# A sandwiched attention and feed-forward layer on eight cores: weight groups of 512 columns taken one at a time instead of in pairs, and the first LayerNorm in groups of three tiles

## The reference

```python
x = x + _layernorm(attn(_layernorm(x), qkv_w, proj_w, proj_b))
x = x + _layernorm(ffn(_layernorm(x), weight, gamma, beta, ln_weight, ln_bias))
# attn: 32 heads of 64, window of 8 tokens to each side with a distance mask,
#       softmax, times v, then out @ proj_w.T + proj_b
# ffn:  xn = layernorm(x) * ln_weight + ln_bias
#       out = xn @ sign(weight).T * max(abs(weight)) * gamma + beta
```

## Time and profile before

| | us |
|---|---|
| median of 3 runs | 1724.91 |
| lowest and highest | 1721.75, 1785.68 |
| the profiled execution | 1722.84 |
| its span, slowest core (core 4) | 1721.3 |
| spans of all cores | 1705.6 to 1721.3 |

### The profile page before, as it was taken

The page is one execution under the profiler, slowest core; times in us unless marked ns, Lnnn a source line. Parts: engine busy times, 40 slices in busy tenths (PEclk is TensorE's granted clock), DMA queues, the critical chain, the costliest instruction groups (busy, mean ns, idle before and its releaser), DMA issues. The chain is left out here.

```text
span 1721.3 us, 12664 instructions; the slowest of 8 cores (1705.6 to 1721.3 us)
## 1 busy us (share of the span) xinstructions
PE 932.3 (54%) x4372; PEld 436.7 (25%) x4432; DVE 570.5 (33%) x820; ACT 305.2 (18%) x438; POOL 306.9 (18%) x207
## 2 busy tenths in 40 slices
PE   1267777776395937766766761949100444249000
PEld 1123333333142413333333330424000222114000
DVE  3611111121202033333243222122527455640565
ACT  2400000000000013222232320000405221230121
POOL 0000000000000044654555540000000222200432
PEclk9998989999697965555555555979655666679555
DMA  3232322221802000000000008140586014040223
GB/s 101 98 123 101 117 100 98 98 98 57 285 1 98 1 28 1 0 1 0 1 0 1 1 0 258 60 147 1 169 290 248 6 43 147 1 146 1 98 97 146
DMA packets 37872, 140.57 MB, mean 82 GB/s; under 512 B 2082, under 2 KB 2082, under 8 KB 27170
## 3 DMA queue, kind: packets, MB, share of 16 engines
q1 hardware_dynamic: 34498, 117.61, 20.2%
q0 software_dynamic: 3312, 22.15, 3.2%
HBM read 122.98 MB, written 16.78 MB: 81 GB/s over the span
## 5 line engine op out<-in xcount | busy, mean ns | idle before, releaser
L379 PE MATMUL qk<-lnT,wbf 128*128 128x512 bf16 (+1 forms) x1254 | 254.5, 359 | 82.1 <-DVE wbf L40 80.2
L379 PEld LDWEIGHTS qk<-lnT,wbf 128*128 128x128 bf16 x1280 | 110.9, 101 | 225.7 <-issue 124.3
L446 PE MATMUL vp<-vwbf,lnT 128*128 128x512 bf16 x565 | 128.2, 388 | 57.1 <-DVE vwbf L40 56.5
L725 PE MATMUL dp<-pwbf,lnT 128*128 128x512 bf16 x501 | 113.9, 388 | 59.7 <-DVE pwbf L40 59.1
L969 PE MATMUL tpe<-identb,lnbf 128*128 128x128 bf16 x128 | 14.9, 308 | 225.0 <-DVE lnbf L955 221.3
L877 PE MATMUL ep<-fwbf,xnT 128*128 128x512 bf16 x500 | 117.5, 394 | 25.9 <-ACT fwbf L846 23.1
L486 POOL DMA_DIRECT2D maskm<-masks x1 | 0.7, 674 | 607.8 <-PE sp L510 607.8
L510 PE MATMUL sp<-KT,QT 64*128 64x144 bf16 x256 | 50.7, 274 | 107.2 <-DVE tstrip L525 101.1
L41 ACT COPY ptbuf<-tpc 128x512 bf16<-128x512 bf16 (+1 forms) x128 | 67.2, 577 | 180.9 <-PE tpc L603 180.9
L567 DVE TENSOR_REDUCE stats<-tstrip 128x16 f32<-128x2304 f32 x16 | 40.8, 2553 | 156.8 <-ACT tstrip L564 156.8
L535 POOL TENSOR_TENSOR tstrip<-tstrip,maskb 128x288 f32<-128x288 f32 x128 | 88.5, 727 | 6.6 <-DVE tstrip L525 6.6
(11 more groups left out here) (94 smaller groups left out, 1007.2 us busy)
## 6 DMA issues: line engine op xcount, KB each, us to landing
wstage<-qk_strips SPq DMA_DIRECT2D x32, 1024.0 KB, 5.9
vstage<-v_w SPq DMA_DIRECT2D x8, 2048.0 KB, 10.8
pwstage<-proj_wt SPq DMA_DIRECT2D x8, 2048.0 KB, 10.8
fwstage<-ffn_wt SPq DMA_DIRECT2D x8, 2048.0 KB, 13.4
ybuf<-y_scratch SPq DMA_DIRECT2D x16, 1024.0 KB, 7.7
xbuf<-x_shard SPq DMA_DIRECT2D x8, 1024.0 KB, 6.1
xre<-x_shard SPq DMA_DIRECT2D x8, 1024.0 KB, 10.6
y_scratch<-x POOLq DMA_DIRECT2D x8, 1024.0 KB, 9.2
```

Source lines behind the costliest of these rows:

```text
L379: return lambda e: e.matmul(banks[gi][:, 0:wd], wbf[:, par * D + kc * 128: par * D + (kc + 1) * 128], lnT[:, kc * TOK + c0: kc * TOK + c0 ...
L446: return lambda e: e.matmul(vbanks[bb][:], lnT[:, kc * TOK + 128 * vt: kc * TOK + 128 * vt + 128], vwbf[:, j * NGV + kc * 512: j * NGV + ( ...
L725: return lambda e: e.matmul(dbanks[bb][:], lnT[:, kc * TOK + 8 + 128 * t: kc * TOK + 8 + 128 * t + 128], pwbf[:, j * NGP + kc * 512: j * N ...
```

## The change

Stages 3, 5, 6 and 7 take one column group of 512 at a time. A pass over the token tiles now has 16 matmuls per tile, all into one bank, and there are two banks in place of four; the two halves of `vwbf`, `pwbf` and `fwbf` are used in turn, and each is released on its own. There are four passes where there were two. In stage 6 only group 0 is staged ahead and multiplied in the pair loop. Groups 1 and 2 follow behind the loop with a staging and a full pass each, then group 3's staging, the scale, and its pass in four pieces. Stage 1 has three buffers and takes the tiles in groups of three, three and two. The numbers of matmuls, weight loads, casts and DMAs stay as they were.

```diff
-            nc.sbuf_tensor("xbuf", [128, 2 * D], F32) as xbuf,
-            nc.sbuf_tensor("lnbf", [128, 2 * D], BF16) as lnbf,
-            nc.sbuf_tensor("sqdump", [128, 2 * D], F32) as sqdump,
+            nc.sbuf_tensor("xbuf", [128, 3 * D], F32) as xbuf,
+            nc.sbuf_tensor("lnbf", [128, 3 * D], BF16) as lnbf,
+            nc.sbuf_tensor("sqdump", [128, 3 * D], F32) as sqdump,
...
-            for bpair in range(0, NT, 2):
-                bs = [bpair, bpair + 1]
-                xas, lbs, cqs = [], [], []
-                for b in bs:
-                    par = b % 2
+            groups = [[0, 1, 2], [3, 4, 5], [6, 7]]
+            xbuf_rd_v = [xbuf_rd_v[0], 0, 0]
+            xbuf_rd_s = [xbuf_rd_s[0], 0, 0]
+            lnbf_rd_t = [lnbf_rd_t[0], 0, 0]
+            for bs in groups:
+                xas, lbs, cqs, pars = [], [], [], []
+                for idx, b in enumerate(bs):
+                    par = b % 3
...
-            nc.psum_tensor([128, 512], F32) as vp2,
-            nc.psum_tensor([128, 512], F32) as vp3,
         ):
-            vbanks = [vp0, vp1, vp2, vp3]
+            vbanks = [vp0, vp1]
...
-            for np_ in range(2):
+            for ng in range(4):
+                par = ng % 2
                 cast_last = 0
-                p.wait("v", "t", vwbf_rd_t)
-                for j in range(2):
-                    ng = np_ * 2 + j
-                    for hh in range(2):
+                p.wait("v", "t", vwbf_rd_t[par])
+                for hh in range(2):
...
                 p.wait("t", "v", cast_last)
...
-                    for kc in range(16):
-                        for j in range(2):
-                            def mk(vt=vt, kc=kc, j=j, bb=b0 + j):
-                                return lambda e: e.matmul(
-                                    vbanks[bb][:],
...
+                        def mk(vt=vt, kc=kc, par=par, bpar=bpar):
+                            return lambda e: e.matmul(
+                                vbanks[bpar][:],
+                                lnT[:, kc * TOK + 128 * vt: kc * TOK + 128 * vt + 128],
+                                vwbf[:, par * NGV + kc * 512: par * NGV + (kc + 1) * 512],
+                                start=(kc == 0), stop=(kc == 15))
+                        last_mm = p.emit("t", mk())
+                    eng = "v" if (vt % 2 == 0) else "s"
+                    p.wait(eng, "t", last_mm)
+                    if eng == "s":
+                        p.wait(eng, "g", c_zero)
+                    def mkevac(vt=vt, ng=ng, bpar=bpar):
+                        return lambda e: _copy(e, 
+                            VTOK[:, vt * D + ng * 512: vt * D + (ng + 1) * 512],
+                            vbanks[bpar][:])
+                    c = p.emit(eng, mkevac())
+                    bank_rd[bpar] = (eng, c)
+                vwbf_rd_t[par] = last_mm
```

The hunk for the output projection is the same edit with `dbanks`, `pwbf` and eight tiles. For the feed-forward stage:

```diff
-            ebanks = [ep0, ep1, ep2, ep3]
-            ebank_rd = [("v", 0)] * 4
+            ebanks = [ep0, ep1]
+            ebank_rd = [("v", 0), ("v", 0)]
...
-            def emit_ffn_mms(np_, tlist):
-                p.wait("t", "s", estate["sign_last"][2 * np_])
-                p.wait("t", "s", estate["sign_last"][2 * np_ + 1])
+            def emit_ffn_mms(ng, tlist):
+                par = ng % 2
+                p.wait("t", "s", estate["sign_last"][ng])
                 p.wait("t", "t", p.cnt["t"])
...
+                    eng = "v" if (t % 2 == 0) else "s"
+                    p.wait(eng, "t", mm_last)
+                    def mkev(t=t, ng=ng, bpar=bpar):
+                        return lambda e: _copy(e,
+                            ffnstage[:, t * D + ng * 512: t * D + (ng + 1) * 512],
+                            ebanks[bpar][:])
+                    c = p.emit(eng, mkev())
+                    ebank_rd[bpar] = (eng, c)
+                    ffn_rdy.setdefault(t, []).append((eng, c))
+                fwbf_rd_t[par] = max(fwbf_rd_t[par], mm_last)
 
             emit_ffn_stage(0)
-            emit_ffn_stage(1)
...
-            emit_ffn_stage(2)
+            for ng in range(1, 3):
+                emit_ffn_stage(ng)
+                emit_ffn_mms(ng, list(range(NT)))
             emit_ffn_stage(3)
...
             for tpair in range(0, NT, 2):
-                emit_ffn_mms(1, [tpair, tpair + 1])
+                emit_ffn_mms(3, [tpair, tpair + 1])
                 ffn_done_pair[tpair] = (p.cnt["v"], p.cnt["s"])
```

More of the change, by code:

```diff
@@ new lines, in build_program, with mkc @@
+                for hh in range(2):
+                    slot = (ng * 2 + hh) % 2
+                    p.wait("q", "v", stage_rd_v[slot])
+                    cq = p.dma("q", lambda e, ng=ng, slot=slot, hh=hh: e.dma_start(
+                        out=vstage[:, slot * NHV:(slot + 1) * NHV],
+                        in_=v_w.rearrange("(k pp) o -> pp k o", pp=128)[
+                            :, hh * 8:(hh + 1) * 8, ng * 512:(ng + 1) * 512]))
+                    p.wait("v", cq)
+                    def mkc(par=par, hh=hh, slot=slot):
+                        return lambda e: _copy(e,
+                            vwbf[:, par * NGV + hh * NHV: par * NGV + (hh + 1) * NHV],
+                            vstage[:, slot * NHV:(slot + 1) * NHV])
+                    cast_last = p.emit("v", mkc())
+                    stage_rd_v[slot] = cast_last
@@ L744, in build_program, with mk @@
-                pwbf_rd_t = mm_last
+                        def mk(t=t, kc=kc, par=par, bpar=bpar):
+                            return lambda e: e.matmul(
+                                dbanks[bpar][:],
+                                lnT[:, kc * TOK + 8 + 128 * t: kc * TOK + 8 + 128 * t + 128],
+                                pwbf[:, par * NGP + kc * 512: par * NGP + (kc + 1) * 512],
+                                start=(kc == 0), stop=(kc == 15))
+                        mm_last = p.emit("t", mk())
@@ new lines, in build_program @@
+                    p.wait("v", "t", mm_last)
+                    p.wait("v", projb_q)
+                    def mkev(t=t, ng=ng, bpar=bpar):
+                        return lambda e: e.scalar_tensor_tensor(
+                            x1[:, t * D + ng * 512: t * D + (ng + 1) * 512],
+                            dbanks[bpar][:], 1.0,
+                            projb[:, ng * 512:(ng + 1) * 512],
+                            ALU.mult, ALU.add,
+                            accum_out=accD[:, t * 4 + ng: t * 4 + ng + 1])
@@ L867, in emit_ffn_mms @@
                 for t in tlist:
[L868 to L871 removed]
+                    bpar = t % 2
+                    eng_r, cnt_r = ebank_rd[bpar]
+                    p.wait("t", eng_r, cnt_r)
                     for (eng_x, c_x) in xnT_rdy[t]:
@@ L874, in emit_ffn_mms @@
                     for kc in range(16):
-                        for j in range(2):
-                            def mk(t=t, kc=kc, j=j, bb=b0 + j):
-                                return lambda e: e.matmul(
-                                    ebanks[bb][:],
-                                    xnT[:, kc * 1024 + 128 * t: kc * 1024 + 128 * t + 128],
-                                    fwbf[:, j * NGF + kc * 512: j * NGF + (kc + 1) * 512],
-                                    start=(kc == 0), stop=(kc == 15))
-                            mm_last = p.emit("t", mk())
```

152 lines of the change are left out of this document (45 added, 107 removed).

## The result

| | before | changed |
|---|---|---|
| median, us | 1724.27 | 1681.52 |
| lowest and highest, us | 1721.75, 1785.68 | 1675.91, 1725.76 |
| runs | 10 | 10 |
| profiled execution, us | 1722.84 | 1678.68 |
| its span (slowest core), us | 1721.3 (core 4) | 1677.1 (core 7) |

The ratio is 0.9733, with a 95% interval of 0.9702 to 0.9763: the change is faster by 2.7%. The forecast was 1675 us, with a range of 1661 to 1692. In some executions the cores of one die show a lower granted clock (0.70 against 0.73 in the one of 1725.76 us) and take longer; medians count these, ratios and intervals leave them out.

The account below looks back on a forecast made before the run. No engine is full; a stage-to-stage chain with TensorE waits sets the end. Gains of 5.6 (first LayerNorm), 13.6 (V), 14.1 (output projection) and 14.6 (feed-forward) sum to 47.9 us: 1722.8 - 47.9 = 1675, range 1661 to 1692.

Parts of the forecast that it names:

- First LayerNorm: First LayerNorm: tiles in groups of 3, 3, 2 let the stage end 5.6 us earlier, bounds 0 to 8.
- V's start: V projection: the first pass needs two weight casts, not four, so it starts 12.5 us earlier.
- Pauses: Both projections: three pauses between passes, about 5.35 us each, replace one of 21.40 (V) or 21.93 (output projection).
- Restarts: Both projections: two extra restarts at the low clock behind pauses cost 2.1 us each, bounds 0 to 2.5.
- Output projection's start: Output projection: TensorE starts behind the second cast, at most at 1061.3 for 1073.96, a gain of 12.6 us.
- Feed-forward start (a): Feed-forward start: one weight group fetched ahead of the y tiles, not two; 12.4 us earlier, bounds 8 and 14.
- Front (b, c): Feed-forward front: (b) each of four pairs has 32 matmuls, not 64, gaining 27.6 us; (c) DVE's sums overlap TensorE, 3.6.
- Behind the front (d, e): After the front: (d) three stagings and passes cost 32.8 us; (e) the tail's first DVE product comes 3.8 earlier.
- 1: Rival: the clock outlasts pauses of 5 to 8 us, so six extra restarts cost nothing; 1662 us, chance 0.08.
- 2: Rival: loads bound the starts, so the first LayerNorm and the feed-forward start gain nothing; 1693 us, chance 0.12.
- 3: Rival: with two banks, late evictions pause TensorE and the clock drops within passes, costing 42 us; 1717 us, chance 0.06.
- 4: Rival: 16 matmuls in a row into one bank go at latency, 0.388 for 0.216 us; 1950 us, chance 0.04.

Follow-up runs that it names:

- filler: The changed kernel with 22 more matmuls, into an unread bank, behind each of the first three passes of both projections; median 1679.17 us, ratio 0.9681.
- four single-part kernels: Four kernels, each the kernel before with one part of the change (first LayerNorm, V projection, output projection, feed-forward); medians 1721.04, 1711.81, 1711.27, 1709.38 us.
- banks4: The changed kernel with four PSUM banks in turn again in V, output projection and feed-forward; median 1682.85 us, ratio 0.9715.
- combo: The changed kernel with projection casts inside the pass before, y tiles loaded first, and later feed-forward groups' signs and maxima moved earlier; median 1588.70 us, ratio 0.9216.
- only_vproj: The kernel before with only the V projection taking one column group at a time; median 1711.81 us, ratio 0.9875.

## Why the prediction was right, point by point

The forecast of 1675 against 1681.52 is off by 6.5 us; as gains, 47.9 was forecast and the medians differ by 42.8. The profiled executions differ by 44.2, the means of their eight spans by 47.1. Between the last two the gap is the choice of the slowest core: core 7, the slowest now, spanned 1721.2 before, and of its 44.1 us less its own tail took back 4.3 (126.1 to 130.4) where the others' moved by 0.2 on average. The mean of the eight cores itself was 1665.4 to 1671.4 in the executions of 1675.91 to 1684.34 us, so a gain read from one profile is good to a few us. The rows of the table sum to within about 1 us of their forecasts, and that is in part luck: single rows miss by up to 1.8 us, in both directions, and the misses nearly cancel. Step by step:

- **First LayerNorm, 5.6: too high by 1.7.** Most of this is the row I started from. The last pair began at 74.90 on core 4, but at 73.6 in the mean of eight cores. The changed kernel's groups began at 27.1, 50.2 and 69.7 in that mean where I had 26.9, 49.6 and 69.2, so the steps hold and the loads add half a us: 6.75 us passed from the first group's last apply to the second group's start, and I had let 5.8 pass. From core to core the stage gained 1.8 (core 3) to 7.0 us (core 4, the one I had read); a sum from one core's rows can miss by that much here.
- **V's start, 12.5: measured 12.6.** The first matmul stands 0.15 behind the second cast, as worked out.
- **Pauses, 5.35 each: exact but for one in V.** 5.35, 5.70 and 5.35 in V, 5.36 three times in the output projection. The weights were hidden, as the cast block at 477.14 shows.
- **Restarts, 2.1 each: right, and now known to be the clock.** The passes are 1.5 to 3.0 us above their pace, and `filler` takes 1.9 a pause back. Pauses and restarts together gave 0.0 in V for a forecast of 1.15, and 0.8 in the output projection for 1.5. The sentence "No pause of 5 us is in the trace" is true of the dense stages alone: in the attention of core 4, 15 pauses of 4.97 to 5.73 us stand ahead of matmuls of 64x144. These come four at a time, so the price of a restart of a long pass couldn't be read from them.
- **Output projection's start, 12.6: measured 13.3.**
- **Feed-forward start (a), 12.4: measured 13.5**, within its bounds.
- **Front (b, c), 31.2: measured 29.4.** (c) was exact: ACT's eviction started at 1312.27 and DVE's step at 1316.75, 4.48 behind (forecast 4.5). The three waits between pairs are 1.24 us shorter each, 3.7 together for 3.6. What was missed is in (b), "the cold part lies in the first 32, so it stays". In the mean of eight cores the four trains of 64 took 59.8 us, 4.5 above the pace of 55.3; the four of 32 take 34.2, 6.5 above 27.6. So 25.6 was gained and not 27.6. Windows of the first 32 matmuls of a pair (PE only, clock in the column behind the count), first of the kernel before, core 4, first and second pair:

```profile
1350.40:1359.60 9.20, 8.93 (x32) 0.77 0.00 0
1399.90:1408.30 8.40, 8.26 (x32) 0.85 0.00 0
```

  then of the changed kernel, the first pair on core 7 and on core 5:

```profile
1303.10:1312.20 9.10, 9.01 (x32) 0.78 0.00 0
1302.90:1310.60 7.70, 7.61 (x32) 0.92 0.00 0
```

  The same 32 matmuls take 7.6 to 9.1 us, as the granted clock has it. Before, core 4 got quicker from pair to pair (7.25 in the last, 14.16 - 6.91), while on cores 0 and 5 the last train of 64 was the longest, 16.1 behind 14.5. Now core 7 takes 9.01, 8.87, 8.79 and 8.76, and core 5 gets slower, from 7.65 to 8.58. So one core's rows don't give this term, and what sets the moment at which the clock rises in a train stays open.
- **Behind the front (d, e), -32.8 + 3.8 = -29.0: measured -27.5.** The pauses are 8.06 (forecast 8.1), each with a restart behind it, and the waits between pieces 0.26, not 0.37. The restart was less than I had it, 29.60 - 27.79 = 1.8 and 8.80 - 7.07 = 1.7 for 2.1. (e): the product stands 2.75 ahead of the last matmul's end (1549.42), forecast 2.7. The scale hid behind the fourth pass.
- **What doesn't change:** Q/K 0.3, attention 0.1, the LayerNorm behind the output projection 1.2, which no part explains: the four single-part kernels have 63.2 to 64.5 there.

The rivals: **1** (the clock outlasts the pauses, 1662) is refuted; a restart follows every pause of 5.35 and 8.06, and `filler` shows its price. **2** (starts bound by loads, 1693) is refuted for both starts: 13.5 us came where 12.4 was forecast, and 3.9 where 5.6 was; of the missing 1.7 the loads account for 0.5. **3** (two banks let the clock drop inside a pass, 1717) is refuted by `banks4`, and by the clock of 1.00 throughout a pass of `filler`. **4** (one bank's accumulation in a row runs at latency, 1950) is refuted: 144 matmuls, 16 in a row to a bank, took 31.24 us in `filler` and 128 took 27.79 in `combo`, 0.217 each.

## What to carry to other kernels

Halving the unit of work that must be staged took 12.6 to 13.5 us off each of three waits of 33 to 43, and that was 39 of the 47 us; the gain from more, shorter passes in the middle was nearly nothing, since each shorter pause was followed by a restart at the lower clock that cost about 2 us. The larger prize was in the order of one engine's list: the same casts placed between the evictions of the pass before, and not behind its last, took pauses and restarts away together, 41.6 us. Look which loads stand ahead of the first one needed, and cut the trace at the same marks on all cores where a few us matter: the slowest core's time moved by 8 us from run to run in the changed kernel (1675.91 to 1684.34) and by 21 in the kernel before (1721.75 to 1743.01), and a part of this change brings 3.5 to 15.4.

## What the runs showed that I had not expected

- Of neighbouring cores (0 and 1, 2 and 3, and so on) the one that comes to the V projection later (counted from its own start) waits longer for the same two weight pieces: in the changed kernel the even cores waited 18.9 to 19.8 us and the odd, later, ones 22.4 to 22.5. In `only_vproj` the first of each pair (1, 3, 4 and 6) waited 18.1 to 18.6 and the second 21.1 to 21.9. So a core that is late falls back by another 3 us at such a stage; what the two share was not tried.
- Between two passes the clock can be kept without the next weights being any earlier: 22 matmuls of no use, 4.91 us of them, did it at no cost that the stages show.
- The parts' medians don't add up (54.5 against 42.8), mostly because the kernel before measured 2.7 us slower in their runs; their stages nearly do (45.6 against 46.9).
- The tail, whose code is untouched, took 125.5 to 130.4 us from core to core here, and up to 133.3 in `banks4`.
